# A graph network on split fp32 products: high halves first, another order of the first sweep and of the last rows, parameters in two loads

## The chip, the cores and the metric

One core of a Trainium2 chip runs the kernel. The metric is the device time of one execution in microseconds (us). Lower is better. Engines are named as in the profile: PE is TensorE (PEld its weight loads), DVE VectorE, ACT ScalarE, SP the queue that issues all DMAs.

## The reference, cut to what matters

All matrices are fp32. `x` is 4096x128 and `adj` 4096x4096. What is computed is a chain of six passes over the same `adj`:

```
x = layernorm(x + relu((adj @ x) @ W0 + b0))          # pass 0, "gcn"
u = x
for _ in range(3):
    v = mlp(adj @ u, uv weights)                      # passes 1, 3, 5
    u = mlp(adj @ v, vu weights)                      # passes 2, 4 (the last u is not needed)
x = layernorm(x + v)
```

`mlp` is three 128x128 layers, each with a bias and a leaky relu. Layernorm is over the 128 features of a row.

## The kernel before

**Blocks.** Rows and columns of `adj` are cut into 8 chunks of 512, so that `adj` is 64 blocks of 512x512. A block is 1 MB, loaded in two *halves* of 512 KB into a ring of six raw buffers (`adj_raw`, `RAW`). Each half is split into `adj_hi` (an ACT copy to fp32r, L526) and `adj_lo` (DVE: raw minus high, L638), and the features are held in the same way as `feat_hi` and `feat_lo`. Split blocks stand in a ring of five slots (`RING`).

**Products.** One product of a block with a chunk of features is 4 ticks. A tick is three matmuls of 512 columns: hi by hi (L646), adj_lo by feat_hi (L647), adj_hi by feat_lo (L648), in the helper `product`. There are 384 products, so 1536 ticks, and PE walks them in the order that `block_products` yields, without a break between passes. "finish r c" adds block (r, c) into row r of sweep s. "begin r c" uses the same block again, while it is in a slot, for the next pass (whose rows are numbered from the other end). A row that has had all its products is *closed*, and becomes a *unit*: for pass 0 its aggregate goes through one small product (pre_ps, L678), bias, relu, residual and layernorm, and the result is split into new features. For the other passes it goes through three layers (hid1, hid2, pre).

**Order on the engines.** Nothing is scheduled by hardware here. Each engine's program is a loop over ticks t. At each tick it first does the steps of units that `plan.steps` puts there (the dictionary `STEPS` gives them in ticks after the row's closing, and units are at least `SPACING` = 10 ticks apart), and then, on ACT and DVE, the splits of all halves whose `due` is at or before t. `due` is 12 ticks ahead of the first use (4 in the first 24 products), or when the slot comes free. SP issues halves in order, and half h waits until adj_lo of half h - 6 is done:

```
if h >= RAW:
    sp.wait_ge(adj_lo_ready, h - RAW + 1)
```

PE, at a product's first use of a half, waits for `adj_lo_ready` (which implies adj_hi). It also waits for the features of a chunk at its first use, and does the unit's matmuls at their ticks before the tick's product. So each engine is an in-order queue, and a step that waits holds back whatever stands behind it.

**The places that the change touches.** In sweep 0 rows 0, 1 and 2 are taken side by side: columns 7 to 3 of these three rows in turn, then the list `FIRST_CORNER`. The chunks of `x` (256 KB each, `brings_x`) are loaded with the first block of their column. Products 0 to 26 all need a fresh block; product 27 is the first that uses one again. Rows 0, 1 and 2 close with products 20, 22 and 23. All parameters (450 KB of weights, 192 KB of broadcast biases) are loaded ahead of half 42 (`LOAD_PARAMS`). The four hidden-layer matrices are split at tick 120 (`W_SPLIT`). The first and last row of each hidden sweep have the steps `TURN`. In the last sweep the rows after row 7 and row 0 go 6, 5, 4, 3, 2, 1. Row 2 there has the steps `LATE`, and row 1, in two halves, `END`. The normalised rows of the last sweep are written by ACT (L448, `act_norm`) from the one buffer `post`, which the next unit's prelu (`act_post`, L427) overwrites and so waits for.

Of the kernel before, what the change touches and what calls it, by code (L numbers as in the profile page):

```python
# [9 lines left out]
P = 128  # L10
# [19 lines left out]
SIDE_BY_SIDE = 3  # L30
FIRST_CORNER = (("finish", 0, (2,)), ("finish", 1, (2,)), ("finish", 2, (2,)), ("finish", 0, (1,)), ("finish", 1, (1,)), ("finish", 0, (0,)), ("finish", 2, (1,)), ("finish", 1, (0,)), ("finish", 2, (0,)), ("finish", 3, (7, 6, 5)), ("begin", 1, (0,)), ("begin", 2, (0,)), ("finish", 3, (4,)), ("begin", 2, (1,)), ("finish", 3, (3,)), ("both", 3, (0, 1, 2)))
LEAD, FIRST_LEAD, FIRST_ROWS = 12, 4, 3
LOAD_PARAMS = 42
W_SPLIT = 120

IN_PARTS, TURN, LATE, END = "in_parts", "turn", "late", "end"
# [4 lines left out]
    TURN: dict(dve_sum=0, act_in=0, dve_in=0, pe_hid1=4, act_hid1=7, dve_hid=6, pe_hid2=9, act_hid2=11,  # L41
# [16 lines left out]
def block_products(rows):  # L58
# [20 lines left out]
    for s in range(PASSES - 1):  # L79
        if s == 0:  # L80
            for c in range(top, SIDE_BY_SIDE - 1, -1):
                for r in range(SIDE_BY_SIDE):
                    yield s, FINISH, r, c
            for what, r, columns in FIRST_CORNER:
                yield from dict(finish=finish, begin=begin, both=both)[what](s, r, columns)
            for r in range(SIDE_BY_SIDE + 1, top):
                yield from finish(s, r, range(r + 1, rows))
                yield from finish(s, r, (r,))
                yield from both(s, r, range(r))
# [21 lines left out]
    for r in range(top - 1, 0, -1):  # L111
        yield from finish(s, r, range(r, -1, -1))


class Plan:


    def __init__(self, rows):
# [36 lines left out]
        for u, (s, r, tiles) in enumerate(self.units):  # L155
            n = self.closes[self.group_of(u)]
            if tiles[0] == 0:
                t = max(t + (SPACING if self.steps_of(u) != END else 1), (n + 1) * TILES)
            after_last = {"dve_pre": ends.get("dve_stats", -1), "act_post": ends.get("act_norm", -1),
                          "act_std": ends.get("dve_shift", -1)} if tiles[0] == 0 else {}  # L160
# [51 lines left out]
    def steps_of(self, u):  # L212
# [3 lines left out]
        if s == PASSES - 1:  # L216
            after = len(self.units) - len(END_UNITS) - u
            return END if after <= 0 else LATE if after == 1 else LAST
        return TURN if r in (0, self.rows - 1) else IN_PARTS

# [28 lines left out]
def gnn_kernel(nc, x, adj, weights, bias_rows, out):  # L249
# [8 lines left out]
    OUT_W = {GCN: 4, UV: 5, VU: 6, LAST: 5}  # L258
# [3 lines left out]
    with ctx:  # L262
# [130 lines left out]
        def ends(u):  # L393
            return u - LAST_0
# [370 lines left out]
```

## Time and profile before

| | us |
|---|---|
| median of 3 runs | 1184.89 |
| lowest, highest | 1182.91, 1185.09 |
| the profiled execution, its own time | 1184.28 |
| its span in the trace | 1182.5 |
| PE busy | 1157.3 (98%), 5220 matmuls and as many weight loads |
| DVE busy | 738.1 (62%) |
| ACT busy | 661.8 (56%) |
| moved by DMA | 261.61 MB, mean 221 GB/s |

Matmuls overlap, so their mean durations (390 ns) are longer than the distance from one to the next. Where PE "sits idle" the cause is read from the row's bracket, which names what ended the wait.

### The profile page before, as it was taken

The page shows a single profiled execution, that of the slowest core. Times are in us where ns is not written, and L with a number is a line of the kernel's source. Part 1 is how long each engine was busy: PE and PEld are TensorE (multiplying, and loading weights), DVE is VectorE, ACT ScalarE, POOL GpSimd, SP SyncE. Part 2 cuts the span into 40 slices and gives each one's busy share as a digit, 9 for nine tenths or more (in the row PEclk, how much of TensorE's full clock was granted, in tenths as well). Part 3 has the DMA queues.
Part 4 walks back from the last instruction along what each step waited for, and adds up shares of the span by engine and source line. Part 5 has one row for each costly group of instructions (what it writes and reads, how often), then busy time and mean ns, then how long its engine had stood idle before and what let it go on. Part 6 is the DMA issues. An engine that isn't in the chain of part 4 may idle for free.

```text
span 1182.5 us, 13669 instructions
## 1 busy us (share of the span) xinstructions
PE 1157.3 (98%) x5220; PEld 951.0 (80%) x5220; DVE 738.1 (62%) x885; ACT 661.8 (56%) x815; POOL 0.2 (0%) x4
## 2 busy tenths in 40 slices
PE   7999999998999999999999999999999999999996
PEld 5777888887888888888888888888888888887775
DVE  7988765458465545665555646544565555668985
ACT  7865544246555545554545645543556544657884
POOL 0000000000000000000000000000000000000000
PEclk9999999999999999999999999999999999999999
DMA  9996766567266556655647635655564656569891
GB/s 363 404 344 237 266 222 218 191 230 251 105 200 208 192 183 209 218 181 193 205 170 247 219 138 177 214 185 190 199 246 159 214 183 227 173 249 348 305 340 45
DMA packets 73073, 261.61 MB, mean 221 GB/s; under 512 B 8112, under 2 KB 8496, under 8 KB 73008
## 3 DMA queue, kind: packets, MB, share of 16 engines
q1 hardware_dynamic: 73008, 260.74, 63.1%
q8 instruction: 41, 0.67, 0.2%
q14 instruction: 24, 0.20, 0.1%
HBM read 258.61 MB, written 2.10 MB: 220 GB/s over the span
## 4 chain that ended last, share of the span: by engine, by line
PE 87%; DMA 6%; DVE 4%; ACT 2%; issue 1%; ACTq 0%; SPq 0%; DVEq 0%
PE agg_ps L646 26%; PE agg_ps L648 26%; PE agg_ps L647 26%; DMA adj_raw<-in_adj 6%; PE pre_ps L678 3%; DVE adj_lo L638 3%; PE hid_ps L646 1%; PE hid_ps L648 1%; PE hid_ps L647 1%; ACT adj_hi L526 1%; PE hid_ps L690 1%; DVE stats L536 0%; ACT resid L448 0%; PE hid_ps L704 0%; ACT hid L427 0%
## 5 line engine op out<-in xcount | busy, mean ns | idle before, releaser
L638 DVE TENSOR_TENSOR adj_lo<-adj_raw,adj_hi 128x1024 fp32r<-128x1024 f32 x488 | 577.9, 1221 | 240.8 <-ACT adj_hi L526 236.8
L646 PE MATMUL agg_ps<-adj_hi,feat_hi 128*128 128x512 f32 x1536 | 610.9, 398 | 11.9 <-DVE adj_lo L638 11.7
L648 PE MATMUL agg_ps<-adj_hi,feat_lo 128*128 128x512 f32 x1536 | 599.7, 390 | 0.0
L647 PE MATMUL agg_ps<-adj_lo,feat_hi 128*128 128x512 f32 x1536 | 599.1, 390 | 0.0
L526 ACT ACTIVATE adj_hi<-adj_raw 128x1024 fp32r<-128x1024 f32 x488 | 492.5, 1052 | 80.1 <-DMA adj_raw<-in_adj 76.7
L646 PEld LDWEIGHTS agg_ps<-adj_hi,feat_hi 128*128 128x128 f32 x1536 | 288.9, 188 | 79.5 <-issue 13.1
L647 PEld LDWEIGHTS agg_ps<-adj_lo,feat_hi 128*128 128x128 f32 x1536 | 289.2, 188 | 61.0 <-issue 3.4
L648 PEld LDWEIGHTS agg_ps<-adj_hi,feat_lo 128*128 128x128 f32 x1536 | 288.8, 188 | 61.2
L427 ACT ACTIVATE hid<-hid_ps,params 128x512 f32<-128x512 f32 (+1 forms) x80 | 54.4, 681 | 78.2 <-PE hid_ps L648 64.1
L492 ACT ACTIVATE in_hi<-part 128x512 fp32r<-128x512 f32 x24 | 15.2, 634 | 103.2 <-DVE part L627 103.2
L427 ACT ACTIVATE post<-pre 128x512 f32<-128x512 f32 (+1 forms) x41 | 25.3, 620 | 80.9 <-DVE pre L607 80.4
L627 DVE TENSOR_TENSOR part<-part,agg_ps 128x512 f32<-128x512 f32 (+1 forms) x31 | 20.6, 666 | 64.5 <-PE agg_ps L648 64.5
L607 DVE TENSOR_TENSOR pre<-pre_ps,b_row 128x512 f32<-128x512 f32 (+1 forms) x48 | 32.8, 684 | 44.1 <-PE pre_ps L678 44.1
L678 PEld LDWEIGHTS pre_ps<-params,hid 128*128 128x128 f32 x380 | 50.8, 194 | 4.9 <-ACT hid L427 0.9
L678 PE MATMUL pre_ps<-params,hid 128*128 128x128 f32 x380 | 51.2, 278 | 0.5 <-ACT hid L427 0.5
L492 ACT ACTIVATE in_hi<-agg_ps 128x512 fp32r<-128x512 f32 x8 | 4.8, 594 | 51.2 <-PE agg_ps L648 51.2
L620 DVE TENSOR_TENSOR in_lo<-agg_ps,in_hi 128x512 fp32r<-128x512 f32 x8 | 5.5, 690 | 44.1 <-ACT in_hi L492 44.1
L615 DVE TENSOR_TENSOR hid_lo<-hid,hid_hi 128x512 fp32r<-128x512 f32 x32 | 22.0, 687 | 15.1 <-ACT hid L427 15.1
L514 ACT ACTIVATE part<-agg_ps 128x512 f32<-128x512 f32 x30 | 17.9, 597 | 23.5 <-PE agg_ps L648 19.9
L503 ACT ACTIVATE hid<-agg_ps 128x512 f32<-128x512 f32 x8 | 4.7, 590 | 46.7 <-PE agg_ps L648 46.7
L427 ACT ACTIVATE hid_hi<-hid_ps,params 128x512 fp32r<-128x512 f32 x32 | 21.8, 681 | 10.5 <-PE hid_ps L648 10.5
L597 DVE TENSOR_TENSOR feat_lo<-post,feat_hi 128x512 fp32r<-128x512 f32 x32 | 22.0, 687 | 8.6 <-ACT feat_hi L427 8.6
(52 smaller groups left out, 261.7 us busy)
## 6 DMA issues: line engine op xcount, KB each, us to landing
adj_raw<-in_adj SPq DMA_DIRECT2D x488, 512.0 KB, 5.7
resid<-in_x SPq DMA_DIRECT2D x8, 256.0 KB, 6.3
out<-resid SPq DMA_DIRECT2D x7, 256.0 KB, 5.1
params<-in_weights SPq DMA_DIRECT2D x1, 450.0 KB, 6.8
out<-resid SPq DMA_DIRECT2D x2, 128.0 KB, 1.7
b_row<-in_bias_rows SPq DMA_DIRECT2D x1, 192.0 KB, 8.0
```

The lines of the kernel that those rows point to most:

```text
L427: return act.activation(to, of, ACT.Prelu, alpha=SLOPE, **bias)
L492: act.activation(in_hi[:, :], agg(u), ACT.Copy).then_inc(in_hi_ready, 1)
L526: act.activation(adj_hi[:, plan.slot[b], i * CHUNK:(i + pieces) * CHUNK], adj_raw[:, h % RAW, 0:pieces * CHUNK], ACT.Copy).then_inc(adj_hi ...
L597: dve.tensor_tensor(feat_block(feat_lo, u), post[:, :], feat_block(feat_hi, u).bitcast(F32), ALU.subtract).then_inc(feat_lo_ready, 1)
L607: dve.tensor_tensor(by_tile(pre[:, own(u)]), by_tile(layer_bank(2, u)), b_row[:, b * P:(b + 1) * P].rearrange("p (j f) -> p j f", f=P) .to ...
L615: dve.tensor_tensor(hid_lo[:, :], hid1[:, :], hid_hi[:, :].bitcast(F32), ALU.subtract)\
L627: dve.tensor_tensor(agg(u), agg(u), agg_bank(u), ALU.add).then_inc(sum_kept, 1)
L638: dve.tensor_tensor(adj_lo[:, plan.slot[b], slot], adj_raw[:, h % RAW, 0:pieces * CHUNK], adj_hi[:, plan.slot[b], slot].bitcast(F32), ALU. ...
L646: pe.matmul(to, l_hi, r_hi, start=start, stop=False)
L647: pe.matmul(to, l_hi, r_lo, start=False, stop=False)
L648: return pe.matmul(to, l_lo, r_hi, start=False, stop=stop)
L678: last = pe.matmul(layer_bank(2, u)[:, k * P:(k + 1) * P], hid2[:, j * P:(j + 1) * P], w_raw[:, OUT_W[kind_of(u)], :], start=True, stop=True)
```

## The change

Six edits, told by what they do:

1. **High first.** PE no longer calls `product` for a tick. In each half block (two ticks) it does hi by hi and adj_hi by feat_lo for both tiles, waiting only for `adj_hi_ready` (and, before the feat_lo product, for the low features), and then the two products with adj_lo, waiting for `adj_lo_ready` ahead of them.
2. **Sweep 0** up to row 6 follows a written list, `FIRST`. Counted along it: products 0 to 24 need fresh blocks, 25, 27 and 29 use one again; rows 0, 1 and 2 close with products 19, 24 and 26 (unit steps begin at ticks 80, 100 and 110, before at 84, 94 and 104); chunks of `x` come with products 0, 2, 3, 7, 9, 10, 18 and 19 (before 0, 3, 6, 9, 12, 15, 18 and 20). From product 44 on, the order of sweep 0 to sweep 4 is that of before. 244 blocks are loaded in both.
3. **Parameters in two parts.** Columns for pass 0 (64 KB of weights, 64 KB of broadcast bias) ahead of half 42, the rest (386 KB and 128 KB) ahead of half 90. The matrices are reordered for that, and their split moves from tick 120 to 320.
4. **TURN.** act_hid1 from tick 7 to 5, dve_hid from 6 to 4. pe_hid1 (4), pe_hid2 (9) and the rest stay.
5. **Last rows** go 6, 5, 4, 3, 1, 2. Row 3 gets the new steps `LATE2`, row 1 the shortened `LATE`, row 2 is `END` (three products to its closing, where row 1 had two).
6. **Buffers of the end.** `END` units write `post_of(u)`, a free stretch of `part`, in place of `post`, so their prelu no longer waits for the norm of the unit before. `normed` and `out_ready` are replaced by two semaphores, one for units normalised on DVE and one for ACT; no entry of `STEPS` puts a unit of the last sweep on DVE, so that branch is not taken. By the plan, the norm of `LATE` now stands at tick 1536, before all END steps of ACT (before at 1547, after END's second layer).

```diff
+FIRST = (("finish", 0, (6,)), ("finish", 1, (6,)), ("finish", 0, (7, 4)), ("finish", 2, (6, 7)),
+         ("finish", 1, (7,)), ("finish", 0, (5,)), ("finish", 1, (5,)), ("finish", 0, (2,)),
+         ("finish", 2, (3, 4, 2)), ("finish", 1, (4,)), ("finish", 3, (5,)), ("finish", 0, (3,)),
+         ("finish", 1, (3, 2)), ("finish", 0, (1, 0)), ("finish", 2, (1,)), ("finish", 1, (0,)),
+         ("finish", 3, (6,)), ("finish", 2, (5,)), ("finish", 1, (1,)), ("begin", 1, (0,)), ("both", 2, (0,)),
+         ("finish", 3, (4,)), ("begin", 2, (1,)), ("finish", 3, (3, 7)), ("finish", 4, (0,)), ("both", 3, (0,)),
...
-LOAD_PARAMS = 42
-W_SPLIT = 120
+LOAD_GCN, LOAD_PARAMS = 42, 90
+W_SPLIT = 320
...
-    TURN: dict(dve_sum=0, act_in=0, dve_in=0, pe_hid1=4, act_hid1=7, dve_hid=6, pe_hid2=9, act_hid2=11,
+    TURN: dict(dve_sum=0, act_in=0, dve_in=0, pe_hid1=4, act_hid1=5, dve_hid=4, pe_hid2=9, act_hid2=11,
...
-    LATE: dict(dve_sum=0, act_in=0, pe_hid1=2, act_hid1=2, pe_hid2=4, act_hid2=5, pe_out=6, dve_pre=8,
-               act_post=8, dve_stats=10, act_std=12, dve_shift=13, act_norm=14),
+    LATE2: dict(dve_sum=0, act_in=1, pe_hid1=4, act_hid1=5, pe_hid2=6, act_hid2=7, pe_out=8, dve_pre=10,
+                act_post=10, dve_stats=12, act_std=14, dve_shift=15, act_norm=16),
+    LATE: dict(dve_sum=0, act_in=1, pe_hid1=1, act_hid1=1, pe_hid2=2, act_hid2=4, pe_out=4, dve_pre=6,
+               act_post=6, dve_stats=7, act_std=7, dve_shift=8, act_norm=9),
...
+LAST_ROWS = (6, 5, 4, 3, 1, 2)
...
+        def post_of(u):
+
+            if plan.steps_of(u) == END:
+                return part_of(chunk_of(plan.first_of(u) - 1))
+            return post
...
+                if h == LOAD_GCN:
+                    sp.dma_start(params[:, 0:P], weights[:, 0:P]).then_inc(gcn_loaded, 16)
+                    sp.dma_start(b_row[:, 0:P], bias_rows[0:P].partition_broadcast(P)).then_inc(gcn_loaded, 16)
                 if h == LOAD_PARAMS:
-                    sp.dma_start(params[:, :], weights).then_inc(params_loaded, 16)
-                    sp.dma_start(b_row[:, :], bias_rows.partition_broadcast(P)).then_inc(params_loaded, 16)
+                    sp.dma_start(params[:, P:], weights[:, P:]).then_inc(params_loaded, 16)
+                    sp.dma_start(b_row[:, P:], bias_rows[P:].partition_broadcast(P)).then_inc(params_loaded, 16)
...
-                last = product(group_bank(g), (feat_hi[feats][:, tile], feat_lo[feats][:, tile]),
-                               (adj_hi[:, plan.slot[b], piece], adj_lo[:, plan.slot[b], piece]),
-                               start=plan.opens[n] and i == 0, stop=plan.closes[g] == n and i == TILES - 1)
+                start = plan.opens[n] and i == 0
+                stop = plan.closes[g] == n and i == TILES - 1
+
+                pe.matmul(group_bank(g), feat_hi[feats][:, tile(src, i)], adj_hi[:, plan.slot[b], piece(i)],
+                          start=start, stop=False)
+                if i == 0 and b in plan.brings_x and s == 0 and into == FINISH:
+                    pe.wait_ge(x_lo_ready, plan.xs.index(c) + 1)
+                if made > n_feats:
+                    pe.wait_ge(feat_lo_ready, made)
+                    n_feats = made
+                pe.matmul(group_bank(g), feat_lo[feats][:, tile(src, i)], adj_hi[:, plan.slot[b], piece(i)],
+                          start=False, stop=False)
                 if i % 2 == 1:
+                    if h > h_lo:
+                        h_lo = h
+                        pe.wait_ge(adj_lo_ready, h + 1)
+                    for k in (i - 1, i):
+                        last = pe.matmul(group_bank(g), feat_hi[feats][:, tile(src, k)],
+                                         adj_lo[:, plan.slot[b], piece(k)], start=False, stop=stop and k == i)
                     last.then_inc(half_used, 1)
```

## Rows read from the trace of the kernel before

**Rows 1.** Windows: busy time and instructions by engine, granted clock, DMA share, GB/s.
```profile
7.30:10.60 3.30, 3.23 (x8) 2.38 (x9) 1.86 (x2) 2.59 (x3) 0.00 (x0) 1.00 1.01 406
...
16.98:59.67 42.69, 42.22 (x182) 33.18 (x180) 39.77 (x35) 34.47 (x35) 0.00 (x0) 1.00 1.02 401
...
72.00:75.20 3.20, 3.20 (x13) 2.85 (x12) 2.34 (x3) 2.77 (x3) 0.00 (x0) 0.50 1.03 375
...
65.58:94.28 28.70, 24.68 (x108) 19.60 (x109) 24.27 (x46) 17.05 (x21) 0.00 (x0) 0.94 0.88 313
94.28:141.47 47.19, 47.19 (x214) 39.19 (x212) 37.74 (x59) 28.17 (x34) 0.00 (x0) 1.00 0.71 245
300.00:1000.00 700.00, 699.71 (x3190) 580.54 (x3189) 393.60 (x398) 368.96 (x457) 0.00 (x0) 1.00 0.57 194
...
```

**Rows 2.** Timeline of the start: start us, duration us, engine, line, operation, idle before.
```profile
4.91 1.06 ACT L526 ACTIVATE adj_hi<-adj_raw 128x1024 fp32r<-128x1024 f32 x1 [0.84 <-DMA adj_raw<-in_adj]
...
7.37 0.76 PE L646 MATMUL agg_ps<-adj_hi,feat_hi 128*128 128x512 f32 x1 [7.37 <-DVE adj_lo L638]
```

**Rows 3.** Timeline of PE in a steady stretch.
```profile
13.04 0.39 PE L646 MATMUL agg_ps<-adj_hi,feat_hi 128*128 128x512 f32 x1
13.26 0.39 PE L647 MATMUL agg_ps<-adj_lo,feat_hi 128*128 128x512 f32 x1
13.49 0.39 PE L648 MATMUL agg_ps<-adj_hi,feat_lo 128*128 128x512 f32 x1
```

**Rows 4.** Groups of PEld instructions: busy us, mean ns, idle before.
```profile
L647 PEld LDWEIGHTS agg_ps<-adj_lo,feat_hi 128*128 128x128 f32 x1536 | 289.2, 188 | 61.0 <-issue 3.4
```

**Rows 5.** Page: DMA issues; chain that ended last, near 60 us.
```profile
params<-in_weights SPq DMA_DIRECT2D x1, 450.0 KB, 6.8
...
59.67 8.32 DMA adj_raw<-in_adj
```

**Rows 6.** Timeline of PE where it waited, 70 to 92 us.
```profile
70.39 0.50 PE L646 MATMUL agg_ps<-adj_hi,feat_hi 128*128 128x512 f32 x1 [1.80 <-DVE adj_lo L638]
...
91.90 0.50 PE L646 MATMUL agg_ps<-adj_hi,feat_hi 128*128 128x512 f32 x1 [1.37 <-DVE adj_lo L638]
```

**Rows 7.** Timeline of DVE, 87 to 95 us.
```profile
87.00 0.68 DVE L607 TENSOR_TENSOR pre<-pre_ps,b_row 128x512 f32<-128x512 f32 x1
87.60 1.22 DVE L638 TENSOR_TENSOR adj_lo<-adj_raw,adj_hi 128x1024 fp32r<-128x1024 f32 x1
88.73 0.69 DVE L582 SCALAR_TENSOR_TENSOR post<-pre,resid 128x512 f32<-128x512 f32 x1
...
94.74 1.22 DVE L638 TENSOR_TENSOR adj_lo<-adj_raw,adj_hi 128x1024 fp32r<-128x1024 f32 x1
```

**Rows 8.** Timeline of PE and ACT at the first turn, 287 to 295 us.
```profile
287.49 0.47 PE L646 MATMUL hid_ps<-in_hi,w_hi 128*128 128x512 f32 x1 [0.77 <-DVE in_lo L620]
...
291.44 1.06 ACT L526 ACTIVATE adj_hi<-adj_raw 128x1024 fp32r<-128x1024 f32 x1 [0.22 <-DMA adj_raw<-in_adj]
292.41 0.67 ACT L427 ACTIVATE hid_hi<-hid_ps,params 128x512 fp32r<-128x512 f32 x1
...
294.60 0.47 PE L646 MATMUL hid_ps<-hid_hi,w_hi 128*128 128x512 f32 x1 [2.74 <-DVE hid_lo L615]
```

**Rows 9.** Timeline of PE, ACT and DVE at the end.
```profile
1161.71 0.39 PE L646 MATMUL agg_ps<-adj_hi,feat_hi 128*128 128x512 f32 x1
...
1169.61 0.39 PE L648 MATMUL agg_ps<-adj_hi,feat_lo 128*128 128x512 f32 x1
...
1171.31 0.47 ACT L427 ACTIVATE hid<-hid_ps,params 128x256 f32<-128x256 f32 x1 [0.78 <-PE hid_ps L704]
...
1173.66 1.64 ACT L448 ACTIVATE resid<-post,shift,rstd 128x128 f32<-128x128 f32 x4
...
1174.65 0.42 DVE L607 TENSOR_TENSOR pre<-agg_ps,b_row 128x256 f32<-128x256 f32 x1
...
1175.67 0.72 ACT L427 ACTIVATE post<-pre 128x256 f32<-128x256 f32 x2 [0.37 <-ACT resid L448]
```

More of the change, by code:

```diff
@@ L80, in block_products @@
         if s == 0:
[L81 to L84, printed above, removed]
+            for what, r, columns in FIRST:
                 yield from dict(finish=finish, begin=begin, both=both)[what](s, r, columns)
[L86 to L89, printed above, removed]
         else:
@@ L110, in block_products @@
     yield from finish(s, top, (0,))
-    for r in range(top - 1, 0, -1):
+    for r in LAST_ROWS:
         yield from finish(s, r, range(r, -1, -1))
@@ L217, in steps_of, with on_vector @@
             after = len(self.units) - len(END_UNITS) - u
-            return END if after <= 0 else LATE if after == 1 else LAST
+            return END if after <= 0 else LATE if after == 1 else LATE2 if after == 2 else LAST
         return TURN if r in (0, self.rows - 1) else IN_PARTS
+    def on_vector(self, u):
+        return "dve_norm" in STEPS[self.steps_of(u)]
     def in_parts(self, u):
@@ L397, in norms, with normed_by, wait_for_normed @@
             return u if u < C else u - LAST_0 + C
+        def normed_by(u, vector):
+            return sum(kind_of(i) in (GCN, LAST) and plan.on_vector(i) == vector for i in range(u + 1))
+        def wait_for_normed(engine, u):
+            if u >= LAST_0:
+                if normed_by(u, True) > C:
+                    engine.wait_ge(dve_normed, normed_by(u, True))
+                if normed_by(u, False):
+                    engine.wait_ge(act_normed, normed_by(u, False))
+        def post_of(u):
+            if plan.steps_of(u) == END:
+                return part_of(chunk_of(plan.first_of(u) - 1))
+            return post
         def at(t, step, kinds):
@@ L465, in _ @@
                     act.wait_ge(pre_ready, u + 1)
-                    if ends(u):
-                        act.wait_ge(out_ready, ends(plan.first_of(u)))
-                    prelu(post[:, own(u)], pre[:, own(u)]).then_inc(post_ready, 1)
+                    if plan.steps_of(u) != END:
+                        wait_for_normed(act, u - 1)
+                    prelu(post_of(u)[:, own(u)], pre[:, own(u)]).then_inc(post_ready, 1)
                 u = at(t, "act_hid2", DEEP)
@@ L535, in statistics @@
                 for j in tiles_of(u):
-                    last = dve.bn_stats(stats[:, j, :], post[:, j * P:(j + 1) * P])
+                    last = dve.bn_stats(stats[:, j, :], post_of(u)[:, j * P:(j + 1) * P])
                 last.then_inc(stats_ready, 1)
@@ L588, in _ @@
                     dve.wait_ge(post_ready, deep(u) + 1)
-                    dve.tensor_tensor(post[:, own(u)], post[:, own(u)], resid[:, columns_of(u)], ALU.add)\
+                    dve.tensor_tensor(post_of(u)[:, own(u)], post_of(u)[:, own(u)], resid[:, columns_of(u)], ALU.add)\
                        .then_inc(total_ready, 1)
@@ L689, in _ @@
                     else:
-                        last = pe.matmul(layer_bank(1, u), w_raw[:, w, :], hid1[:, own(u)], start=True, stop=True)
+                        last = pe.matmul(layer_bank(1, u), w_hid[:, w, :], hid1[:, own(u)], start=True, stop=True)
                     last.then_inc(hid2_done, 1)
@@ L703, in _ @@
                         pe.wait_ge(sum_kept, plan.sums(u))
-                        last = pe.matmul(layer_bank(0, u), w_raw[:, w, :], agg(u), start=True, stop=True)
+                        last = pe.matmul(layer_bank(0, u), w_hid[:, w, :], agg(u), start=True, stop=True)
                     else:
                         pe.wait_ge(agg_kept, plan.kept(u))
-                        last = pe.matmul(layer_bank(0, u), w_raw[:, w, :], hid1[:, own(u)], start=True, stop=True)
+                        last = pe.matmul(layer_bank(0, u), w_hid[:, w, :], hid1[:, own(u)], start=True, stop=True)
                     last.then_inc(hid1_done, 1)
@@ L752 @@
               for tag in ("uv", "vu"))
-    matrices = [uv["W1"], uv["W2"], vu["W1"], vu["W2"], L0_gnn_kernel, uv["W3"], vu["W3"]]
+    matrices = [L0_gnn_kernel, uv["W1"], uv["W2"], vu["W1"], vu["W2"], uv["W3"], vu["W3"]]
     bias_columns = [_np.asarray(b).reshape(P, 1) for b in (uv["b1"], uv["b2"], vu["b1"], vu["b2"])]
```

73 lines of the change are left out of this document (42 added, 31 removed).

## The prediction

> **What bounds the kernel now.** I read the windows first. From 300 to 1000 us PE is busy for 699.71 of 700 us and DVE for 393.6 [rows 1]: in the middle the kernel is bound by PE, and nothing that this change does to waits can help there. So I look for time only at the start, at the first turn of sweeps and at the end. A tick's three matmuls start 0.22 to 0.23 us apart [rows 3], which over a long stretch comes to 0.2267, so that a product (12 matmuls) takes 2.72 us and a pass-0 unit's eight small matmuls 0.9. The 17 products and one unit from 94.28 to 141.47 us are 17 x 2.72 + 0.9 = 47.2, just the width of that window, PE busy throughout [rows 1].
>
> At the start PE does nothing until 7.37, and its release is adj_lo [rows 2]. Its first matmuls are slow, 8 in 3.23 us (0.40 each), though the granted clock reads 1.00 there [rows 1]. From 17 to 60 us the DMA engines are at a share of 1.02 and 401 GB/s [rows 1]: a block of 1.049 MB arrives every 2.62 us, a chunk of x adds 0.66. Three blocks and a chunk are 8.5, three products only 8.16, so DMA sets the pace. Product 20 starts at 65.58 and product 27 at 94.28 [rows 1]: 28.70 us for 7 x 2.72 + 2 x 0.9 to 3 x 0.9 = 21 to 22, so 7 us are lost there. The chain passes through an 8.32 us stretch of DMA that holds the 450 KB of weights [rows 5], PE waits 1.80 and 1.37 us for adj_lo [rows 6], and between the two the granted clock is 0.50 from 72.0 to 75.2 [rows 1]: the lower level, 1.2 GHz, after a stall. DVE is the second half of that loss. From 87.00 to 94.74 it goes without a pause through one unit's worth of work (pre, post, statistics, norm, feat_lo) and three splits [rows 7]. A split follows the last after 1.13 (87.60 to 88.73), so a unit costs DVE 7.74 - 3 x 1.13 = 4.35 us. A fresh product gives DVE 2.26 us of work in 2.72, so each unit that falls among fresh blocks makes it late by up to 4.
>
> At the first turn PE waits 0.77 and then 2.74 us for a unit of its own [rows 8]. At the end, the last matmul starts at 1169.61 [rows 9], so 12.7 us of the span are tail.
>
> **High first.** PE now needs adj_hi of the first half, ready at 4.91 + 1.06 = 5.97 [rows 2], plus 0.15. It starts 1.25 us earlier, and as DMA sets the pace, stays 1.25 ahead. Count and kind of matmuls are the same. Elsewhere adj_lo may come four matmuls (0.9 us) later without a stall.
>
> One thing could speak against it: before, the two products with feat_hi stood side by side on the same weights, now they are apart. But each matmul has a load of its own, 1536 of 188 ns for L647 alone [rows 4], less than the 0.22 to the next matmul, and the step from L646 to L647 (0.22) is not shorter than that from L647 to L648 (0.23) [rows 3]. So I take nothing. The Trainium skill says the opposite in "TensorE: Matmul & The Clock Gate", under Step-by-step, that separate loads let you load once and multiply repeatedly, which would make parting them a loss. By the row it would be none, by the rule, if the pair had shared a load, at most 188 ns of work hidden below a matmul.
>
> **Order of sweep 0 and the parameters.** I follow the written order in four steps.
> (a) Up to product 20, DMA sets the pace. Before, product 20 followed 20 blocks and had all of x with it (65.58). Now 20 blocks and all of x are needed by product 19, so product 20 starts, at no loss, at 65.58 - 1.25 = 64.3. That some chunks of x come earlier (four by product 7) only shifts bytes within this stretch.
> (b) Products 20 to 24 are fresh, and row 0 closed with 19, so 3.8 of its unit's 4.35 us on DVE (all but feat_lo) stand ahead of the split of the last of these blocks. At 64.3 the low half of product 20 is ready at about 65.5. Then come nine splits of 1.13 to 1.22, say 10.8, the 3.8, and 0.8 for DMA, still the slower by little (0.3 of it the 128 KB of parameters, where 642 KB, 1.6 us, stood): 80.9. The last two matmuls of product 24 follow, and product 25 starts at 81.3. If DVE kept up, it would be 64.3 + 5 x 2.72 + 0.9 = 78.8.
> (c) Products 25, 27 and 29 use blocks again, so from there DVE gets air. Product 29 needs unit 1's features, closed four products earlier: 4 x 2.72 + 0.9 = 11.8 us of PE, against 12 ticks of steps (8.2), the 0.9, and DVE's backlog of two or three splits. I take a stall of 0.8, between 0 and 2.
> (d) From 25 to 44 are 19 products and three units: 19 x 2.72 + 3 x 0.9 = 54.4. Product 44 starts at 81.3 + 54.4 + 0.8 = 136.5, before at 141.47 [rows 1]: **5.0 gained**. Bounds: with DVE keeping up and no stall 133.2, 8.3 gained. If the stalls add up to another drop of the clock as at 72 us (1.7) and DVE is late by another 1.7, 139.9, 1.6 gained. I choose near the middle, because the kernel before shows both faults in the same place.
>
> Parameters: SP issues four DMAs where it issued two, about 0.4 each, in a queue that waits for adj_lo anyway. The second pair (514 KB, 1.3 us) comes at half 90, where DMA is at 0.71 or less [rows 1]. The split of the matrices (1.3 us on ACT and DVE) moves from tick 120, inside (c), to 320. Its first user is at tick 384, over 40 us later. Cover there is 6 us by which splits are ahead, and without it 1.3 would be lost. Nothing for either.
>
> **TURN.** At the first turn, ACT did the split at 291.44 and then hid_hi at 292.41, and PE started at 294.60 [rows 8]. With act_hid1 two ticks earlier it stands ahead of that split, due between the two: 1.1 to 1.2 earlier on ACT, DVE and PE. The 0.77 before it stays, as in_lo is not moved. **1.2 gained**, between 0 and 3.5 (both waits). All later waits of the 700 us window are 0.3, so I take 0.2. dve_hid now stands at the same tick as the PE product it waits for, over ACT: DVE stands for about 2.1 us (three matmuls, two prelus of 0.7). Behind it on DVE are splits, and behind these SP's next load. They are 5 us or more ahead of PE there.
>
> **End.** Before, ACT was in L448 (1173.66 to 1175.30) while the last row's pre was there: first prelu at 1175.67, second half's pre at 1174.65, the first half's before that. One us is lost, and the new buffer removes it. In its place, LATE's norm now comes ahead of the last row's first prelu in ACT's queue. Before, LATE closed at 1161.71 and its norm began 11.95 later [rows 9]. Now LATE closes 3 x 2.72 plus its own 0.86 x 2 + 0.9 = 10.8 before PE's end, so at the old pace the norm runs from 1.2 to 2.8 after that end, and the first prelu, before at 1171.31 - 1169.84 = 1.5, waits until 2.8. That is 1.3 lost against 1.0 gained: **-0.3**. Faster LATE steps may save up to the 1.3 (then +1.0), a stall of PE on LATE's hid2, one tick behind hid1, may cost 0.3 and more: -1.3.
>
> **Sum.** 5.0 + 1.2 + 0.2 - 0.3 = 6.1. Span 1182.5 - 6.1 = 1176.4. The profiled execution took 1184.28, 1.8 more than its span and 0.6 less than the median, so the median goes from 1184.89 to **1178.8**.
>
> **Rivals.**
> - *DVE keeps up* (no stall in b and c). For it: four matmuls of new cover. Against: 3.8 us of unit among nine splits. 8.3 + 1.2 + 0.2 + 0 to 1 gives 1175.2 to 1174.2, and with the whole turn 1172.
> - *DVE is the limit in sweep 0 as before*, with another low-clock stretch: 1.6 to 2.5 in place of 5.0, in all about 3.2: 1181.7.
> - *The change doesn't do what it says.* Front 1.6, turn 0, because ACT there waits for DMA and not for its place, end -1.3: 0.3, so 1184.6.
> - *Slower: DVE's early wait in TURN.* There are 8 such units. If splits were ahead by less than the 2.1 us that DVE stands, PE would wait for adj_lo. At 2.1 each, 16.8 lost against 4.9 gained: 1196.8. Against it: DVE is idle for 306 of 700 us [rows 1] and no split is late there. It decides only from a lead under 2.1.
>
> **How the numbers follow.** What can be told from no change is about 0.2%, 2.4 us. Forecast (4 to 8.4 gained): 0.55. DVE keeps up: 0.17. DVE the limit (2.4 to 4 gained): 0.13. Nothing that can be measured: 0.08. Slower, by the TURN wait or by several of the bounds: 0.07. So faster 0.85, same 0.08, slower 0.07. The sum of the best bounds is 13, of the worst 0.3: 1172 to 1184.6. Leaving out the last two cases, the range is 1172.0 to 1183.0. The likeliest case's own is 1176.5 to 1181.
>
> **What would show it.** The first matmul at about 6.1. Product 20 at 64.3 and 25 at 81.3 (78.8 if DVE keeps up), product 44 at 136.5. The waits for adj_lo near 70 to 92 us smaller and no window at clock 0.50. The wait for hid_lo at the first turn down from 2.74 to about 1.6. In the tail L448 standing before the last row's first prelu, and no wait of post on resid. Wrong it would be if PE's windows from 300 to 1000 us were no longer full (spacing or TURN), if product 29 waited long for features, or if x, asked for earlier, starved products 3 to 10 by more than PE later makes up.

## The result, and the profile after

| | before | changed |
|---|---|---|
| median, us | 1184.89 | 1176.78 |
| lowest to highest, 5 runs each | 1182.91 to 1187.24 | 1175.52 to 1179.89 |
| profiled execution, its span | 1184.28, 1182.5 | 1176.77, 1175.0 |

The ratio is 0.9938 with a 95% interval of 0.9922 to 0.9955: 8.1 us faster. The prediction said 1178.8 in a range of 1172 to 1183.

Windows of the changed kernel. The first three answer to [rows 1], the next holds products 20 to 24.

```profile
6.80:10.10 3.30, 3.25 (x8) 2.61 (x9) 2.29 (x2) 2.02 (x2) 0.00 (x0) 1.00 0.98 356
16.98:58.00 41.02, 39.96 (x173) 31.67 (x172) 37.27 (x32) 31.92 (x33) 0.00 (x0) 1.00 1.00 383
72.00:75.00 3.00, 3.00 (x15) 2.48 (x14) 2.96 (x5) 1.56 (x2) 0.00 (x0) 1.00 0.99 381
66.88:84.41 17.53, 15.49 (x70) 11.82 (x68) 16.32 (x27) 12.42 (x14) 0.00 (x0) 1.00 0.90 331
84.41:138.83 54.42, 54.42 (x254) 45.50 (x252) 44.70 (x76) 31.78 (x39) 0.00 (x0) 1.00 0.74 253
300.00:1000.00 700.00, 700.00 (x3197) 582.11 (x3197) 393.15 (x398) 368.42 (x455) 0.00 (x0) 1.00 0.57 195
```

PE now idles 1.1 us between 17 and 58, where it idled 0.5 between 17 and 60 before, and DMA brings 383 GB/s in place of 401. The window at clock 0.50 near 72 us is gone. From product 25 to 44 (84.41 to 138.83) PE never stops: 54.42 us, as the prediction's step (d) has it. The middle is as full as before.

The start, timeline (answers to [rows 2]):

```profile
5.65 1.06 ACT L561 ACTIVATE adj_hi<-adj_raw 128x1024 fp32r<-128x1024 f32 x1 [1.44 <-DMA adj_raw<-in_adj]
...
6.85 0.77 PE L776 MATMUL agg_ps<-adj_hi,feat_hi 128*128 128x512 f32 x1 [6.85 <-ACT adj_hi L561]
```

PE follows the high split by 0.14, but that split starts 0.74 later than before (5.65 against 4.91). The first matmul is 0.52 earlier, not 1.25.

PE's two longest stops among products 20 to 24 (answers to [rows 6]):

```profile
77.30 0.73 PE L790 MATMUL agg_ps<-adj_lo,feat_hi 128*128 128x512 f32 x2 [1.31 <-DVE adj_lo L673]
...
81.11 0.73 PE L790 MATMUL agg_ps<-adj_lo,feat_hi 128*128 128x512 f32 x2 [0.72 <-DVE adj_lo L673]
```

The first turn, timeline (answers to [rows 8]):

```profile
284.84 0.47 PE L681 MATMUL hid_ps<-in_hi,w_hi 128*128 128x512 f32 x1 [0.76 <-DVE in_lo L655]
...
286.76 1.06 ACT L561 ACTIVATE adj_hi<-adj_raw 128x1024 fp32r<-128x1024 f32 x1 [0.41 <-DMA adj_raw<-in_adj]
...
287.72 0.67 ACT L462 ACTIVATE hid_hi<-hid_ps,params 128x512 fp32r<-128x512 f32 x1
...
289.92 0.47 PE L681 MATMUL hid_ps<-hid_hi,w_hi 128*128 128x512 f32 x1 [0.96 <-DVE hid_lo L650]
```

The wait for in_lo is the same (0.76), the one for hid_lo falls from 2.74 to 0.96. From the unit's first matmul to its second layer it is 5.08 us, before 7.11. Two splits start on ACT between them and ahead of hid_hi, before there were three.

The end, timeline (answers to [rows 9]):

```profile
1162.92 0.61 PE L790 MATMUL agg_ps<-adj_lo,feat_hi 128*128 128x512 f32 x2
...
1163.63 1.65 ACT L483 ACTIVATE resid<-post,shift,rstd 128x128 f32<-128x128 f32 x4 [0.44 <-DVE shift L612]
1165.19 0.45 ACT L462 ACTIVATE hid<-hid_ps,params 128x256 f32<-128x256 f32 x1
...
1168.15 0.43 DVE L642 TENSOR_TENSOR pre<-agg_ps,b_row 128x256 f32<-128x256 f32 x1
1168.16 0.86 ACT L462 ACTIVATE part<-pre 128x256 f32<-128x256 f32 x2 [0.83 <-DVE pre L642]
```

LATE's norm (L483) stands before the last row's first prelu, as predicted, and holds it until 1165.19. The last prelus (1168.16) no longer wait for a norm.

Where the time went, by the starts of products in the two traces (us):

| | before | changed | lead |
|---|---|---|---|
| first matmul | 7.37 | 6.85 | 0.52 |
| product 12 | 43.13 | 44.05 | -0.92 |
| product 20 | 65.58 | 66.88 | -1.30 |
| product 25 | 85.14 | 84.41 | 0.73 |
| product 44 | 141.47 | 138.83 | 2.64 |
| product 98, behind the first turn | 298.27 | 293.80 | 4.47 |
| product 300 | 910.10 | 903.95 | 6.15 |
| product 378 | 1148.11 | 1141.55 | 6.56 |
| end of the span | 1182.5 | 1175.0 | 7.5 |

So the total is near the forecast (7.5 in the span, forecast 6.1), but its parts do not agree with it: 2.64 in front where 5.0 were forecast, 1.8 at the first turn (1.2), 2.1 later in the sweeps (0.2), 0.9 at the end (-0.3).

### The profile page after: what moved, and what is told of

It reads as the page before. It is cut to its first block, busy times and chain, and to the rows that moved or that the text cites. A ratio compares the mean times of both kernels' runs of the same rounds, so it can differ in the third digit from the quotient of the medians.

```text
span 1175.0 us, 13669 instructions
## 1 busy us (share of the span) xinstructions
PE 1155.3 (98%) x5220; PEld 950.7 (81%) x5220; DVE 738.4 (63%) x885; ACT 662.4 (56%) x815; POOL 0.2 (0%) x4
## 4 chain that ended last, share of the span: by engine, by line
PE 93%; DMA 3%; DVE 2%; ACT 1%; issue 0%; ACTq 0%; SPq 0%; DVEq 0%
PE agg_ps L790 28%; PE agg_ps L776 28%; PE agg_ps L783 28%; PE pre_ps L719 4%; DMA adj_raw<-in_adj 3%; DVE adj_lo L673 1%; PE hid_ps L681 1%; PE hid_ps L683 1%; PE hid_ps L682 1%; ACT adj_hi L561 1%; PE hid_ps L731 1%; PE hid_ps L745 0%; DVE stats L571 0%; DVE resid L586 0%; ACT resid L483 0%
## 5 line engine op out<-in xcount | busy, mean ns | idle before, releaser
L790 PE MATMUL agg_ps<-adj_lo,feat_hi 128*128 128x512 f32 x1536 | 475.4, 391 | 2.0 <-DVE adj_lo L673 2.0
L462 ACT ACTIVATE hid<-hid_ps,params 128x512 f32<-128x512 f32 (+1 forms) x80 | 54.4, 680 | 65.4 <-PE hid_ps L683 56.0
L462 ACT ACTIVATE post<-pre 128x512 f32<-128x512 f32 x39 | 24.6, 631 | 84.9 <-DVE pre L642 84.9
```

Source lines behind the costliest of these rows:

```text
L462: return act.activation(to, of, ACT.Prelu, alpha=SLOPE, **bias)
L790: last = pe.matmul(group_bank(g), feat_hi[feats][:, tile(src, k)], adj_lo[:, plan.slot[b], piece(k)], start=False, stop=stop and k == i)
```

## The experiments

Two theories stood. The first: the front is late because the chunks of x, asked for early, take DMA from blocks that PE needs. The rival: something else in the new order (the block that is read first, or DVE). "Excess" is by how much a product took longer than its own 2.72 us and the unit work in it.

**u_order: the changed kernel with the order of sweep 0 of before.**
```diff
-            for what, r, columns in FIRST:
+            for c in range(top, SIDE_BY_SIDE - 1, -1):
+                for r in range(SIDE_BY_SIDE):
+                    yield s, FINISH, r, c
+            for what, r, columns in FIRST_CORNER:
```


> The changed kernel with the first sweep in the order of before; all else stays. The changed kernel's trace has product 44 at 138.83 us (before: 141.47) and is 7.5 us of span shorter. Theory: the new order pays, because three pass-0 units no longer fall on fresh blocks at once: without it product 44 comes at 140 to 141 and the span is 1176.5 to 1177.5. Rival: the early chunks of x cost in products 7 to 10 as much as the later closings give back, and high-first alone makes the gain of the front: product 44 at 138 to 139, span within 0.7 of 1175.0. The start tells a third thing: if the first adj_hi is ready at 5.97 as before and not at 6.71, the second chunk of x, issued ahead of half 4, delayed it.

Measured: 1177.47 us, ratio 0.9946 (0.9926 to 0.9967). The first matmul is at 6.12 and product 20 at 64.25, just the 6.1 and 64.3 of the prediction: high first does shift the whole front by 1.3. But product 44 comes at 137.69, 1.1 us before the changed kernel and before what either theory had (140 to 141, 138 to 139). The span of 1175.4 is the rival's: in the whole, the new order is worth nothing that this run shows. From 20 to 44 the old order takes 73.44 us and the new one 71.95. So in these two profiles the new order gains 1.5 behind product 20 and loses 2.6 ahead of it.

**early_x: u_order, with the chunks of x issued ahead of the half blocks at which the new order asks for them.** Nothing else moves.
```diff
+EARLY_X = (0, 4, 6, 14, 18, 20, 36, 38)
...
-                if b in plan.brings_x and i == 0:
-                    c = plan.brings_x[b]
+                if h in EARLY_X:
+                    c = plan.xs[EARLY_X.index(h)]
```


> The changed kernel with the first sweep in the order of before (first matmul at 6.12, product 8 at 30.07, 9 at 32.79, 12 at 41.79, 44 at 137.69, span 1175.4), and in it the eight chunks of x issued ahead of halves 0, 4, 6, 14, 18, 20, 36, 38, where the new order has them, in place of 0, 6, 12, 18, 24, 30, 36, 40. Only SP's order changes. Theory: the second chunk ahead of half 4 delays the first half (first matmul at 6.7 to 6.9), and the chunks ahead of 14, 18 and 20 starve PE near 35 us, which is not made good afterwards as PE then is the slower: product 12 at 43 to 44, product 44 at 138.8 to 139.5. Rival: the stops near 35 us come from the ACT and DVE splits of x, which here stay in their places: product 12 at 42.0 to 42.6, product 44 within 0.7 of 137.7.

Measured: 1180.35 us, 0.9968 (0.9954 to 0.9981). The first adj_hi is there at 5.94 as in u_order (5.98), so SP's order of x does not delay the start. Product 12 is 1.8 us later (43.62 against 41.79), product 20 2.8 (67.05) and product 44 2.4 (140.11). Windows of u_order, then of early_x:

```profile
16.98:58.00 41.02, 40.92 (x176) 32.14 (x175) 38.41 (x34) 33.16 (x34) 0.00 (x0) 1.00 1.03 407
41.79:64.25 22.46, 22.46 (x97) 17.68 (x97) 21.34 (x20) 18.51 (x19) 0.00 (x0) 1.00 1.03 404
```

```profile
16.98:58.00 41.02, 40.01 (x168) 30.71 (x169) 36.52 (x33) 31.92 (x33) 0.00 (x0) 1.00 1.00 381
41.79:64.25 22.46, 22.23 (x95) 17.18 (x94) 19.96 (x19) 17.30 (x19) 0.00 (x0) 1.00 0.99 374
```

PE stops for 1.0 us by 58 where it stopped for 0.1, and DMA moves 6% fewer bytes in the same time (381 for 407 GB/s). Half of that is a lower busy share (1.00 for 1.03), which fits SP's rule: it may not ask for half h before half h - 6 is split, and those splits are later now. The other half is fewer bytes at the same share, and it comes in stretches:

```profile
46.00:54.00 8.00, 7.83 (x35) 6.19 (x34) 6.55 (x7) 5.57 (x7) 0.00 (x0) 1.00 0.94 315
```

The bytes of x alone don't explain 2.8 us. Ahead of product 12 six chunks have been asked for in place of five, which is 0.66 us of DMA, and by product 20 both orders have asked for all eight. So the run shows that the order in which x is asked for costs time, and not why it costs this much.

**col6: u_order with columns 6 and 7 swapped.** A single time, so without an interval.
```diff
-            for c in range(top, SIDE_BY_SIDE - 1, -1):
+            for c in (6, 7, 5, 4, 3):
```


> The changed kernel with the first sweep in the order of before, save that its first two columns change places: the three rows take column 6 first, then 7. So far the first adj_hi was ready at 5.94 to 5.98 in four kernels that begin with block (0, 7), and at 6.58 to 6.99 in six that begin with block (0, 6), although one of the four had the second chunk of x ahead of half 4 too. Theory: it is which blocks (addresses) are read first: ready at 6.6 to 7.0. Rival: it is the order of the chunks of x behind them: ready at 5.9 to 6.0.

Measured: 1179.15 us, span 1177.4. The first split, timeline:

```profile
5.58 1.06 ACT L561 ACTIVATE adj_hi<-adj_raw 128x1024 fp32r<-128x1024 f32 x1 [1.57 <-DMA adj_raw<-in_adj]
```

It ends at 6.64, u_order's at 5.98, with the same count and size of loads in the same order. So it is the block that is read first that costs this 0.7, and not the chunks of x behind it. All seven profiles that begin with block (0, 7) have the split done between 5.88 and 5.98, all seven that begin with (0, 6) between 6.58 and 6.99. By product 20 (64.37, u_order 64.25) all but 0.1 of it is made up here.

**late_x: a third order.** Rows 0 to 2 side by side down to column 2, as before, so that x comes every third product and (0, 7) is first. From product 18 on nearly the new list, with block (3, 5) moved back to product 23.
```diff
+FIRST = tuple(("finish", r, (c,)) for c in (7, 6, 5, 4, 3, 2) for r in (0, 1, 2)) + (
+         ("finish", 0, (1, 0)), ("finish", 2, (1,)), ("finish", 1, (0,)),
+         ("finish", 3, (6, 5)), ("finish", 1, (1,)), ("begin", 1, (0,)), ("both", 2, (0,)),
...
```


> The changed kernel with a third order of the first 24 products: rows 0, 1 and 2 side by side in columns 7 to 2, as before, so that chunks of x come with products 0, 3, 6, 9, 12, 15, 18 and 19; then as in the new order, with (3, 5) at product 23 in place of (2, 5). Rows close with 19, 24 and 26 and blocks are used again from 25, as in the new order. Theory: the new order gains 1.5 us between products 20 and 44 (71.95 against 73.44) and loses 2.6 before 20 by early x and the slower first reads. So product 20 comes at 64.2 to 64.6, product 44 at 136.1 to 136.8, and the span is 1172.3 to 1173.3. Rival: the gain after 20 hangs on what was done before (row 2's late column, block (3, 5) at product 14): product 44 at 137.5 or more, span 1174 or more.

Measured: 1175.66 us, 0.9936 (0.9921 to 0.9950), span 1173.5. First matmul 6.07, product 20 at 64.47, 25 at 81.52, 44 at 135.97. The prediction had 6.1, 64.3, 81.3 and 136.5 for the changed kernel, and this order, which spreads x evenly, meets them in this profile. A second profile of the same front does not (product 20 at 66.48, in best below). In the ratio the two orders can't be told apart (0.9936 and 0.9938), in the span this one is 1.5 ahead.

**u_params: all parameters at half 42 again, matrices split at tick 120.**
```diff
-LOAD_GCN, LOAD_PARAMS = 42, 90
-W_SPLIT = 320
+LOAD_GCN, LOAD_PARAMS = 42, 42
+W_SPLIT = 120
```


> The changed kernel with all parameters loaded ahead of half 42 and the matrices split at tick 120, as before. Changed: product 20 at 66.9, 25 at 84.4, 44 at 138.8, span 1175.0. Theory: 514 KB more at half 42 make halves 42 and on 1.3 us later while DMA still sets the pace, and PE's pause is long enough for the clock to fall: product 25 at 86 to 88, product 44 at 140.5 to 142, span 1177 to 1178.5. Rival: DVE with its unit is the limit there, and the bytes hide behind it: product 44 within 0.4 of 138.8.

Measured: 1179.32 us, 0.9960 (0.9943 to 0.9977). Product 20 comes 0.2 before the changed kernel's, product 44 1.1 later (139.91). The stretch between them takes 73.27 us, and 71.27 to 71.95 in the four profiles that have the changed kernel's front: parting the parameters is worth 1.3 to 2.0 us there, where the prediction had nothing. The theory had the clock fall behind PE's pause, but the granted clock is 1.00 from 66.64 to 85.49.

**u_lowfirst: the three matmuls of a tick together again, all behind adj_lo.**
```diff
-                pe.matmul(group_bank(g), feat_hi[feats][:, tile(src, i)], adj_hi[:, plan.slot[b], piece(i)],
-                          start=start, stop=False)
...
+                last = product(group_bank(g), (feat_hi[feats][:, tile], feat_lo[feats][:, tile]),
...
```


> The changed kernel with hi by hi, adj_lo by feat_hi, adj_hi by feat_lo in each tick as before, and the wait for adj_lo ahead of all. Theory: high-first gives 1.2 us at the start, 0.9 us of cover at each late split in products 8 to 24, and about 0.4 us in each of four sweeps where PE waits for new features: first matmul 1.3 later, product 44 at 141 to 142.5, sweeps 1 to 4 longer by 1 to 1.5 in all, span 1178.5 to 1180. Rival: as the DMA sets the pace the start alone counts, and feature waits are noise: span about 1176.3.

Measured: 1180.01 us, 0.9965 (0.9952 to 0.9977). First matmul 8.12, 1.27 later, which is DVE's split. Product 20 is at 68.13 and product 44 at 139.68, 1.25 and 0.85 later than in the changed kernel's profile and well before the 141 to 142.5 expected, but four profiles of the changed kernel's front differ by more than that (66.05 to 68.35, 137.82 to 139.62). From product 100 to 348 it takes 745.39 us and the changed kernel 744.47. These 0.9 are four stops of 0.24, one in each sweep (the first where product 103 begins), and the weight load there waits for low features. The kernel before has them too:

```profile
315.12 0.19 PEld L646 LDWEIGHTS agg_ps<-adj_hi,feat_hi 128*128 128x128 f32 x1 [0.39 <-DVE feat_lo L597]
```

**only_high: the kernel before with high first alone.** The edit of u_lowfirst the other way round:
```diff
-                last = product(group_bank(g), (feat_hi[feats][:, tile], feat_lo[feats][:, tile]),
...
+                    if h > h_lo:
+                        h_lo = h
+                        pe.wait_ge(adj_lo_ready, h + 1)
```

> The kernel before with the new order of matmuls alone (hi by hi and adj_hi by feat_lo first, adj_lo after; split waits). Before: first matmul 7.37, product 20 at 65.58, product 44 at 141.47, span 1182.5. Theory: high-first gives 1.25 us at the start, keeps it to product 20 (64.3), and covers 0.9 of the splits that come late behind the 642 KB of parameters; product 44 at 138.5 to 140, features cost 0.4 less in each sweep turn, span 1179 to 1180. Rival: the parameters' 1.6 us in the DMA stream still stop PE long enough for the clock to fall (0.50 near 72 us), so that product 44 comes at 140.5 to 141 and the span is 1181.

Measured: 1183.42 us, 0.9990 (0.9979 to 1.0002), nothing that can be told from before. The trace shows why. Product 20 is at 64.23 and 44 at 139.72, a lead of 1.75. Then product 97 at the turn has an excess of 4.52, before 2.94, and 1.6 of the lead is spent there. PE's wait for hid_lo is little longer (2.92, before 2.74), but now the clock falls behind it (0.78 granted from 294.0 to 298.1), which it didn't in the kernel before. In this pair of profiles high first gains time in front and the turn takes it back. Both theories had a shorter span (1179 to 1180, 1181; measured 1182.9).

**u_turn: only TURN as before.**
```diff
-    TURN: dict(dve_sum=0, act_in=0, dve_in=0, pe_hid1=4, act_hid1=5, dve_hid=4, pe_hid2=9, act_hid2=11,
+    TURN: dict(dve_sum=0, act_in=0, dve_in=0, pe_hid1=4, act_hid1=7, dve_hid=6, pe_hid2=9, act_hid2=11,
```

> The changed kernel with act_hid1 at tick 7 and dve_hid at tick 6 of TURN, as before. Theory: the wait for hid_lo at the first turn comes back (excess of product 97 at 2.9 instead of 1.14), and that of product 225 (0.5): 2.3 us, span 1177.3, and the front up to product 96 is unchanged. Rival: the first turn got shorter because splits arrived earlier after the new front, so that TURN's ticks give nothing: span 1175.0 to 1175.5.

Measured: 1182.25 us, 0.9983 (0.9970 to 0.9996), the highest of all kernels that keep the rest of the change. Timeline and window:

```profile
288.89 1.06 ACT L561 ACTIVATE adj_hi<-adj_raw 128x1024 fp32r<-128x1024 f32 x1 [1.72 <-DMA adj_raw<-in_adj]
...
290.19 1.06 ACT L561 ACTIVATE adj_hi<-adj_raw 128x1024 fp32r<-128x1024 f32 x1 [0.24 <-DMA adj_raw<-in_adj]
291.16 0.67 ACT L462 ACTIVATE hid_hi<-hid_ps,params 128x512 fp32r<-128x512 f32 x1
...
293.35 0.47 PE L681 MATMUL hid_ps<-hid_hi,w_hi 128*128 128x512 f32 x1 [3.57 <-DVE hid_lo L650]
```

```profile
293.30:297.00 3.70, 3.65 (x11) 2.94 (x12) 1.64 (x2) 1.28 (x2) 0.00 (x0) 0.66 0.89 328
```

hid_hi needs nothing but the matmuls of the first layer, done long before. In ACT's queue it stands behind these two splits, and each of them waits for its DMA (1.72, 0.24). PE waits 3.57, and about 1 us after it is back the clock falls (0.66 on average, so partly at 1.2 GHz): matmuls are 0.43 apart in place of 0.23. That PE is earlier doesn't explain the longer wait. The load of the first of the two halves is asked for 4.1 us before the unit's first matmul, as in the kernel before and in only_high, but takes 7.4 us to land, there 6.8 and 6.7. Product 97 has an excess of 5.32, in the changed kernel 1.14. Of the two spans' difference of 7.0 that is 4.2. Another 0.8 lies in front, where the two kernels are the same, 0.5 and 0.4 at the turns of later sweeps (products 225 and 289), and 1.1 is not settled. Both expected spans were too short (1177.3, and 1175.0 to 1175.5; measured 1182.0).

**u_end: the last rows, LATE and END as before.**
```diff
-LAST_ROWS = (6, 5, 4, 3, 1, 2)
+            return END if after <= 0 else LATE if after == 1 else LAST
...
-            if plan.steps_of(u) == END:
-                return part_of(chunk_of(plan.first_of(u) - 1))
```


> The changed kernel with the last rows in the order 6 to 1, the old LATE, no LATE2, and END units in the buffer post with its wait. Theory: the tail from the last matmul is 12.7 instead of 11.6 us, while the stretch of the last four products is equal: span 1175.9 to 1176.1. Rival (my prediction's own reckoning): the end lost 0.3 by the norm of LATE ahead of the last row's first prelu, so without it the span is 1174.7.

Measured: 1179.19 us, 0.9959 (0.9945 to 0.9973). From product 379 to the end of the span it takes 31.67 us, the changed kernel 30.73 and the kernel before 31.67. The new end is worth 0.94. The whole span (1177.5) is another 1.6 longer, over both theories, by what lies ahead of it.

**late_dve: the norm of LATE on DVE.** It takes ACT's norm from before the last row's first prelu.
```diff
-               act_post=6, dve_stats=7, act_std=7, dve_shift=8, act_norm=9),
+               act_post=6, dve_stats=7, act_std=7, dve_norm=12),
```


> The changed kernel with the norm of LATE on DVE (dve_norm at tick 12 after closing, behind the first sum of the last row) in place of dve_shift and ACT's act_norm. In the changed kernel DVE is idle for 3.38 us there, and ACT's norm (1163.63 to 1165.28) stands ahead of the last row's first prelu at 1165.19, 1.83 us after PE's end, where it was 1.47 before. Theory: the first prelu comes 0.3 to 0.4 earlier and the tail is 11.2 to 11.4 instead of 11.64 us; span 1174.6 to 1174.8. Rival: ACT was not what the prelu waited for, tail 11.6.

Measured: 1178.12 us, 0.9953 (0.9934 to 0.9972): not to be told from the changed kernel by the median. In the trace the first prelu starts 1.48 behind PE's last matmul (1.83 in the changed kernel), and the tail is 11.30 in place of 11.63. So the norm costs 0.33, not the 1.3 of the prediction.

**best: late_x, LATE's norm on DVE, and act_hid1 of TURN one tick earlier still.**
```diff
-    TURN: dict(dve_sum=0, act_in=0, dve_in=0, pe_hid1=4, act_hid1=5, dve_hid=4, pe_hid2=9, act_hid2=11,
+    TURN: dict(dve_sum=0, act_in=0, dve_in=0, pe_hid1=4, act_hid1=4, dve_hid=4, pe_hid2=9, act_hid2=11,
```

> The kernel with the third order, and with two more edits: the norm of LATE on DVE (tail 11.30 instead of 11.63 us in its own run), and act_hid1 of TURN at tick 4, so that at the first turn ACT does hid_hi ahead of the split that waits longest for DMA. Theory: tail 11.3, excess of product 97 at 0.2 to 0.7 instead of 1.1 to 1.9, span 1171.0 to 1172.3. Rival: ACT, standing at tick 4 for PE, makes the splits behind it late, and PE waits for them in products 98 to 104 or later in the sweeps: those lose what 97 gains.

**old_order_best: best with the order of sweep 0 of before.** The edit is that of u_order.

> The fastest version so far (third order, norm of LATE on DVE, act_hid1 of TURN at tick 4: 1174.54 us, product 44 at 137.83 in its profile) with the first sweep in the order of before. Four profiles of one and the same new front put product 44 at 137.8 to 139.6, two of the third order at 136.0 and 137.8, and one of the old order with high-first and split parameters at 137.7, so a single profile does not tell the orders apart. Theory: closing rows 1 and 2 later is worth 1 to 1.5 us where x is loaded evenly: product 44 at 137.7 to 139, median 1175.3 to 1176.5. Rival: the order of sweep 0 is worth nothing once high-first, split parameters and TURN are there: median 1174.2 to 1175.

Measured: best 1174.54 us, 0.9923 (0.9907 to 0.9938), the fastest of all. old_order_best 1177.52, 0.9949 (0.9933 to 0.9965). Waits of PE for splits and features at the first turn (280 to 300 us), us in total, times, longest: the kernel before, the changed kernel, best:

```profile
PE hid_ps L646 <- DVE hid_lo L615: 2.7, 1, 2.7
PE hid_ps L646 <- DVE in_lo L620: 0.8, 1, 0.8
```

```profile
PE hid_ps L681 <- DVE hid_lo L650: 1.0, 1, 1.0
PE hid_ps L681 <- DVE in_lo L655: 0.8, 1, 0.8
```

```profile
PE hid_ps L679 <- DVE in_lo L653: 0.8, 1, 0.8
```

The wait for hid_lo is gone, and the excess of product 97 is 0.23, as expected. The span (1173.7) is not the 1171.0 to 1172.3 expected, because of the front: best reaches product 20 at 66.48 and product 44 at 137.83, late_x 64.47 and 135.97, with the same instructions up to there. That is how far one profile's front can be trusted. The changed kernel's front has four such profiles too (itself, late_dve, u_end, u_turn): 137.82 to 139.62. The old order has 137.69 and 138.65. So differences of the fronts under 1.9 us are not shown by one profile each. The stretch from product 20 to 44 spreads less: 71.50 and 71.35 with the third order, 73.44 and 73.50 with the old, 71.27 to 71.95 with the new. Best against old_order_best is 3.0 us of median, with intervals that just overlap (0.9907 to 0.9938, 0.9933 to 0.9965); the two profiled spans are only 0.8 apart (1173.7 and 1174.5). Together with that step it is the best sign that the order of sweep 0 is worth something when x comes evenly.

## Why the prediction was right, and where its steps were not

**High first: right.** 6.1 for the first matmul and 64.3 for product 20 came out in u_order at 6.12 and 64.25, and in only_high at 6.10 and 64.23. That the two products with feat_hi are parted costs nothing: an undisturbed product takes 2.72 us in both orders, and u_lowfirst, which has them side by side, is slower. The Trainium skill's sentence on loading once, cited in the prediction, doesn't come to bear: there are 5220 weight loads in both kernels.

**(a) was wrong, by 2.6 us, and why is shown only in part.** It said "some chunks of x come earlier (four by product 7) only shifts bytes within this stretch", at a rate of DMA that it took as given. The sum of bytes up to product 20 is indeed the same, but the rate is not. From 17 to 58 us the seven profiles with early chunks have 375 to 394 GB/s and reach product 20 at 66.0 to 68.4. Of the six others with high first, five have 406 to 409 GB/s and reach it at 64.2 to 65.2. The sixth is best: x spread evenly, 386 GB/s, product 20 at 66.5.

```profile
36.00:42.00 6.00, 6.00 (x28) 4.94 (x27) 5.84 (x6) 5.09 (x6) 0.00 (x0) 1.00 0.93 316
```

So early chunks go with the loss (early_x: 2.8 in one pair), but up to 2.0 of it can come without them. In the changed kernel the slow stretch is 40 to 48 us (310 GB/s), and SP asks for chunks at 27.5 and at 51.9, none between. What slows DMA there stays open. Of the prediction's signs of failure this was the last one, x that starves early products. It happened without turning the result, as the gains behind were larger. The 0.7 for the first block comes on top at the first matmul; in col6 all but 0.1 of it was made up by product 20.

**(b) and (d) were right.** Products 20 to 24 took 17.5 us (forecast 17.0), with DVE busy for 16.3 of them and PE's stops ending on adj_lo. The products from 25 to 44 took 54.4 (54.4). The times themselves were late, product 25 at 84.4 for 81.3, mostly by what (a) had lost. **(c)** was not needed: product 29 had no stall where 0.8 was taken, within the stated 0 to 2. The granted clock never fell in front, where it did before at [rows 1].

**Parameters: mis-sized.** "Nothing for either", measured 1.1 at product 44 in one pair of profiles, 1.3 to 2.0 in the stretch from product 20 to 44, and 2.5 us of median, with intervals that overlap. The 1.3 us of DMA at half 42 was counted only in (b).

**TURN: right in its mechanism, and without the clock.** The forecast of 1.2 takes the excess of product 97 from 2.94 to about 1.7. Nine kernels have the new TURN: seven have 1.6 to 2.0 there, two 1.1, and the changed kernel is one of the two. So its 1.8 is on the lucky side, and 1.2 was a good price for PE's wait. What the prediction left out here is the clock. With the old TURN the excess is 2.94 where the clock held (the kernel before), and 4.52 and 5.32 where it fell (only_high and u_turn, after waits of 2.92 and 3.57). That is how taking TURN out costs 4.2 at this place in one pair of profiles, and 5.5 us of median. The 8 early waits of DVE, the rival on the slower side, did nothing: no split is late there, and PE is busy for 700.00 of 700 us.

**Later sweeps: 2.1 where 0.2 were forecast.** The prediction took PE's 0.3 us of idle time in 700 for all that was to be had. About 1.0 is high first: the four stops of 0.24 named at u_lowfirst, which are gone. They show no idle time on PE, because a matmul stands in the profile for 0.39 us and the next one starts 0.23 after it; only the weight load's row shows the wait. Another 0.55 is the turn at product 225, which took 0.5 longer than its work and now doesn't. The rest lies in parts too small to tell from the spread: product 357 alone has an excess from 0.47 to 2.04 over the runs, and why stays open.

**End: mis-sized.** Forecast -0.3, measured 0.94 (u_end). The 1.0 for the free buffer was right: the last prelu starts 0.46 after its pre, before 1.47. The 1.3 for LATE's norm was 0.33, since LATE's chain ran faster than at "the old pace": the norm started 0.3 behind PE's end, not 1.2. Not in the sum was another 0.4: LATE's std no longer stands between the last row's prelus on ACT, which need 2.51 us to the first pre (before 2.89). The bounds (-1.3 to 1.0) held the total.

The sum was closer than its parts by luck: 2.4 too much was forecast in front and 3.7 too little behind it. Nor do the parts add up: alone, high first is worth nothing (only_high), and TURN 1.2 by the old trace, but without TURN 5.5 of the 8.1 us are gone.

Not tried: a deeper ring of raw halves, which would loosen SP's wait, and an earlier in_lo, whose 0.8 us at the turn is left in every kernel.

## What to carry to other kernels

Where DMA sets the pace and the engine has almost no reserve, an equal sum of bytes doesn't make two orders of loads equal: asking early for x went with 2.8 us in one pair of profiles, more than its bytes account for. So read the rate of DMA in the stretch, and spread extra loads evenly until it is shown that they may come early. Time gained in front lasts only if nothing later takes it back, so look for the next step that waits for the same DMA, and put an engine's short steps on the critical path ahead of work in its in-order queue that waits for a transfer. Price such a step with the clock in mind: a wait of 2.74 us made its product 2.94 longer, one of 2.92 made it 4.52 longer. Take the front of one profile for no more than its spread between equal kernels, here up to 2.3 us. And where a matmul stands in the profile for longer than the step to the next one, look for short waits in the rows of the weight loads.

## What the runs showed of the hardware

- **The first block read.** Reading block (0, 6) first makes the first 512 KB 0.7 us later than (0, 7), in every profile (col6). Each block lies contiguous, 8 KB for each partition, of which a half reads 4. The Trainium skill's "DMA: Bandwidth & Descriptors", under Latency and other measured facts, tells of read rates that fall at row pitches that are large powers of two; here the pitch is the same in both, so that does not explain it. The cause is open.
- **Busy DMA with fewer bytes.** From 44 to 46 us, in windows of the changed kernel and the kernel before:

```profile
44.00:46.00 2.00, 2.00 (x10) 1.65 (x10) 1.96 (x3) 1.40 (x2) 0.00 (x0) 1.00 0.98 252
```

```profile
44.00:46.00 2.00, 2.00 (x11) 1.62 (x10) 1.91 (x3) 1.58 (x3) 0.00 (x0) 1.00 1.02 393
```

  The share is full in both, the rate 252 against 393 GB/s. Five of the six kernels with the new order have 223 to 274 there and one has 346, at shares from 0.85 to 1.06; all others have 390 and more. But slow stretches are not the new order's alone: early_x has one from 46 to 54 (315 GB/s) and best one from 36 to 42 (316). So the busy share alone doesn't tell what DMA moves. The cause is open.
- **The clock.** The granted clock fell to 0.50 after a wait of 1.80 us in the kernel before [rows 6], to 0.78 on average after 2.92 us in only_high and to 0.66 after 3.57 us in u_turn, while after the 2.74 us at the turn of the kernel before it stayed at 1.00 (294.6 to 298.3 us). So the length of the last wait alone doesn't tell whether the clock falls.
